# Second attention of a hybrid network: token routing in five units instead of four, the first two one tile later

## The reference, cut to what matters

```python
# L2, attention then experts, per batch
q, k, v = E @ WQ, E @ WK, E @ WV
# scores below the diagonal alone, softmax over the row, times v, added to E
# layer norm, then:
logits = xn @ gate_w + gate_b            # 128 -> 16
# two largest of 16, weights by softmax of the two
# each expert: silu(x @ w1) * (x @ w2) @ w3, summed with the two weights
```

## Time and profile before

| what | value |
|---|---|
| median of 3 timed runs | 1950.14 us (1949.3 to 1958.3) |
| the profiled execution's own time | 1943.94 us |
| its span in the profile | 1942.1 us |
| mean granted TensorE clock | 0.919 |
| PE busy | 1654.9 us, 85% |
| DVE busy | 1331.3 us, 69% |
| ACT busy | 991.6 us, 51% |
| POOL busy | 331.6 us, 17% |
| indirect DMAs of L1904 | 64, 62.1 us busy |

### The profile page before, as it was taken

How to read it: one execution, slowest core, us unless ns; L and a number is a source line. 1 busy time by engine, 2 the same in 40 slices (tenths; PEclk the granted TensorE clock), 3 DMA queues, 4 the chain that set the end, 5 groups by cost and what they waited for, 6 DMA issues and landing times. The chain is left out here.

```text
span 1942.1 us, 29755 instructions
## 1 busy us (share of the span) xinstructions
PE 1654.9 (85%) x9244; PEld 857.4 (44%) x9244; DVE 1331.3 (69%) x2650; ACT 991.6 (51%) x1857; POOL 331.6 (17%) x329
## 2 busy tenths in 40 slices
PE   5999897899999998598875199846999999996898
PEld 3777443222222223475554188722222222235576
DVE  5763598888888867345777244457888888856665
ACT  2555233366766775004444076642567676775233
POOL 6020400100000001100034545540000000011000
PEclk9999998699999999699998599966899999996899
DMA  3260057025454310104000132139033233310000
GB/s 105 98 143 10 0 150 221 1 49 86 75 87 74 70 48 16 25 1 138 1 23 30 55 97 68 41 133 248 17 57 57 56 56 56 56 37 2 6 17 22
DMA packets 117113, 122.71 MB, mean 63 GB/s; under 512 B 24300, under 2 KB 90324, under 8 KB 115976
## 3 DMA queue, kind: packets, MB, share of 16 engines
q1 hardware_dynamic: 101598, 102.07, 23.3%
q0 software_dynamic: 15408, 19.31, 3.5%
HBM read 79.00 MB, written 41.84 MB: 62 GB/s over the span
## 5 line engine op out<-in xcount | busy, mean ns | idle before, releaser
L944 DVE TENSOR_REDUCE heads_mx<-scales_n_bank 128x1 f32<-128x1024 f32 (+2 forms) x280 | 324.3, 1196 | 60.4 <-PE scales_n_bank L810 59.0
L925 ACT ACTIVATE heads_prob<-scales_t_bank 128x512 f32<-128x512 f32 x512 | 264.5, 603 | 140.2 <-PE scales_t_bank L829 140.2
L944 DVE TENSOR_REDUCE heads_mx<-edge_n_bank 128x1 f32<-128x1024 f32 x256 | 301.4, 1219 | 50.1 <-PE edge_n_bank L810 48.7
L925 ACT ACTIVATE heads_prob<-edge_t_bank 128x512 f32<-128x512 f32 x512 | 264.4, 603 | 133.2 <-PE edge_t_bank L829 133.1
L810 PE MATMUL scales_n_bank<-scale_ks,scale_qs 96*128 96x512 bf16 (+2 forms) x608 | 177.2, 382 | 27.5 <-DVE heads_mx L944 14.2
L810 PE MATMUL edge_n_bank<-edge_ks,edge_qs 99*128 99x512 bf16 x512 | 163.9, 404 | 23.8 <-PEq L43 12.8
L829 PE MATMUL scales_t_bank<-scale_qs,scale_ks 99*128 99x512 bf16 (+2 forms) x608 | 169.0, 365 | 3.6 <-ACT heads_prob L925 3.5
L829 PE MATMUL edge_t_bank<-edge_qs,edge_ks 102*128 102x512 bf16 x512 | 154.8, 382 | 3.5 <-ACT heads_prob L925 3.5
L845 PE MATMUL edge_o_bank<-heads_prob,edge_vs 128*32 128x512 f32 x1024 | 136.4, 605 | 0.1
L845 PE MATMUL scales_o_bank<-heads_prob,scale_vs 128*32 128x512 f32 x1024 | 136.4, 605 | 0.0
L810 PEld LDWEIGHTS scales_n_bank<-scale_ks,scale_qs 96*128 96x128 bf16 (+1 forms) x608 | 46.3, 99 | 174.8 <-issue 98.3
(11 more groups left out here) (365 smaller groups left out, 2700.4 us busy)
## 6 DMA issues: line engine op xcount, KB each, us to landing
edges_text<-edges_targets SPq DMA_DIRECT2D x16, 512.0 KB, 3.6
scale_qs<-scale_q_parts SPq DMA_DIRECT2D x60, 128.0 KB, 4.8
scale_ks<-scale_k_parts SPq DMA_DIRECT2D x60, 128.0 KB, 6.5
heads_wide<-heads_inverse_d POOLq DMA_DIRECT2D x15, 512.0 KB, 10.8
edge_qs<-edge_q_parts SPq DMA_DIRECT2D x48, 128.0 KB, 4.9
edge_ks<-edge_k_parts SPq DMA_DIRECT2D x48, 128.0 KB, 7.4
routed_x<-attn_zeros SPq DMA_DIRECT2D x2, 2600.0 KB, 15.2
experts_xs<-routed_x SPq DMA_DIRECT2D x16, 325.0 KB, 4.4
```

Of the source, the lines that this page charges most:

```text
L925: act.activation(to[:], t_ps[score_bank(of, place, g)[0]][0:TN, 0:HP * CH], ACT.Exp, scale=scale).then_inc(exped, 1)
L944: dve.tensor_reduce(mx[:, u % UC:u % UC + G], scores, AX.X, ALU.max, negate=True).then_inc(first_used, 1)
```

## The change

The routing is cut into five units instead of four. `COUNT` gives their tiles, `FIRST` their first tile. Units 0, 1 and 2 are batches 0, 1 and 2; units 3 and 4 are the two halves of batch 3, four tiles each.

- Units 0 and 1: every part stands one tile later than before, `place_rows` in tile 0 of the batch after. Their eight `normalise` are now four in tile 1 and four in tile 2, and the root alone is in tile 0.
- Unit 2: its parts stand where they stood, but its `place_rows` and `advance` stand ahead of `add_output` in the last tile, and its `note_pages` behind `measure(31)`.
- Unit 3 begins inside the loop: its root in tile 29, `find_shift` in tile 30, `normalise` and `turn_rows` in tile 30. Unit 4 is behind the loop.
- Units 3 and 4 turn their rows into the banks of the score buffer 0, which the last tiles have left free (`turned_ps`); unit 4 keeps its logits and sums in score buffer 1.
- `note_pages` is split: what the next unit needs (`base`, `last_shift`) is the new `advance`. `weigh` is split from `pick`.
- POOL waits once a unit, and scatters 16, 16, 16, 8 and 8 DMAs: 64 as before.

```diff
+    COUNT = [T] * (B - 1) + [T // 2, T // 2]
+    UNITS = len(COUNT)
+    FIRST = [sum(COUNT[:u]) for u in range(UNITS + 1)]
...
-        logits_ps, total_ps, within_ps = (x_ps[:, i * P:(i + 1) * P] for i in range(3))
+        turned_ps = lambda u: x_ps[:] if u < B - 1 else s_ps[0][:, (u - B + 1) * 512:(u - B + 2) * 512]
+        sums_ps = lambda u, i: (x_ps if u < B else s_ps[1])[:, i * P:(i + 1) * P]
...
-            for f in range(B):
-                pool.wait_ge(doubled, f + 1)
-                pool.wait_ge(armed, 2 * (f + 1))
-                pool.wait_ge(placed, f + 1)
-                for t in range(T):
+            for u in range(UNITS):
+                pool.wait_ge(doubled, u + 1)
+                pool.wait_ge(armed, 2 * (u + 1))
+                pool.wait_ge(placed, u + 1)
+                for t in range(COUNT[u]):
...
+            inside, behind = {}, {}
+            for u in range(B - 1):
+                begin = FIRST[u + 1]
+                if u < B - 2:
+                    behind[begin + 2] = (turn_rows, u, 0)
+                    inside[begin + 4], inside[begin + 5], inside[begin + 7] = (turn_rows, u, 1), (gate_logits, u), (count_picks, u)
+                else:
+                    behind[begin + 1] = (turn_rows, u, 0)
+                    inside[begin + 3], inside[begin + 4], inside[begin + 6] = (turn_rows, u, 1), (gate_logits, u), (count_picks, u)
+            behind[B * T - 2] = (turn_rows, B - 1, 0)
...
+            steps = {}
+            for u in range(B - 1):
+                begin = FIRST[u + 1]
+                if u < B - 2:
+                    steps[begin] = ((take_root, u),)
+                    steps[begin + 1], steps[begin + 2] = ((normalise, u, 0, 4),), ((normalise, u, 4, 8),)
+                    steps[begin + 5], steps[begin + 6], steps[begin + 7] = ((double, u),), ((take_odds, u),), ((arm, u),)
+                else:
+                    steps[begin], steps[begin + 1], steps[begin + 2] = ((take_root, u), (normalise, u, 0, 2)), ((normalise, u, 2, 4),), ((normalise, u, 4, 8),)
+                    steps[begin + 4], steps[begin + 5], steps[begin + 6] = ((double, u),), ((take_odds, u), (take_root, B - 1)), ((arm, u), (normalise, B - 1, 0, 4))
+            steps[B * T - 1] = ((take_rows, B - 1, 0), (double, B - 1))
...
+            def advance(u):
+
+                dve.tensor_tensor(base[u + 1][:], base[u][:], ends[u][:, E - 1:E], ALU.add)
+                then(dve.scalar_tensor_tensor(out=change[:], in0=fresh[:], scalar=0.0, in1=change[:], op0=ALU.is_gt, op1=ALU.mult))
+                then(dve.tensor_tensor(last_shift[:], last_shift[:], change[:], ALU.subtract))
...
-            beside = {0: (find_shift,), 4: (choose,), 5: (pick,), 6: (hand_out,), 7: (place_rows,)}
+            beside = {g: [] for g in range(B * T)}
+            for u in range(B - 1):
+                begin = FIRST[u + 1]
+                late = u < B - 2
+                beside[begin + late].append((find_shift, u))
+                beside[begin + 4 + late].append((choose, u))
+                beside[begin + 5 + late] += [(pick, u), (weigh, u)]
+                beside[begin + 6 + late].append((hand_out, u))
+                if late:
+                    beside[begin + 8] += [(place_rows, u), (advance, u)]
+                    beside[begin + 9].append((note_pages, u))
+            beside[B * T - 2].append((find_shift, B - 1))
+            beside[B * T - 1].append((note_pages, B - 2))
+            ahead = {B * T - 1: ((place_rows, B - 2), (advance, B - 2))}
...
+            choose(B - 1)
+            find_shift(B)
+            pick(B - 1)
+            hand_out(B - 1)
+            place_rows(B - 1)
+            weigh(B - 1)
+            advance(B - 1)
+            choose(B)
+            pick(B)
+            note_pages(B - 1)
+            hand_out(B)
+            place_rows(B)
+            weigh(B)
+            note_pages(B)
```

More of the change, by code:

```diff
@@ L1995, in _ @@
                     project(b + 1, early[t])
-                if b >= 1 and t in inside:
-                    inside[t](b - 1)
+                if g in inside:
+                    part, *which = inside[g]
+                    part(*which)
                 mix(g)
@@ L2000, in _ @@
                     project(b + 1, late[t])
-                if b >= 1 and t == 1:
-                    turn_rows(b - 1, 0)
-            turn_rows(B - 1, 0)
-            for part in inside.values():
-                part(B - 1)
+                if g in behind:
+                    part, *which = behind[g]
+                    part(*which)
+            gate_logits(B - 1)
+            count_picks(B - 1)
+            turn_rows(B, 0)
+            gate_logits(B)
+            count_picks(B)
             pe.wait_ge(tabled, 1)
@@ L2031, in keep_turned @@
                 act.activation(probT[g % 2][:, 0:t + 1, :], t_ps[:, 0:t + 1, :], ACT.Copy).then_inc(turn_kept, 1)
-            def take_root(f):
-                act.wait_ge(measured, (f + 1) * T)
-                if f >= 1:
-                    act.wait_ge(shifted, f)
-                act.activation(root[:], mv[:, f * T:(f + 1) * T, 1], ACT.Sqrt, bias=epsb[:]).then_inc(rooted, 1)
-            def normalise(f, first, end):
-                act.wait_ge(shifted, f + 1)
-                for t in range(first, end):
-                    act.activation(rows[:, f * T + t, 0, 0:C], m.tt[:, f * T + t, :], ACT.Identity, bias=shift[:, t:t + 1], scale=rstd[:, t:t + 1]).then_inc(normed, 1)
@@ new lines, in normalise, with take_rows @@
+            def normalise(u, first, end):
+                act.wait_ge(shifted, u + 1)
+                for t in range(first, end):
+                    act.activation(rows[:, FIRST[u] + t, 0, 0:C], m.tt[:, FIRST[u] + t, :], ACT.Identity, bias=shift[:, t:t + 1], scale=rstd[:, t:t + 1]).then_inc(normed, 1)
+            def take_rows(u, half):
+                done = FIRST[u] // 4 + half
+                act.wait_ge(x_turned, done + 1)
+                if u >= 1:
+                    act.wait_ge(logits_made, u if COUNT[u] == T else B - 1)
+                act.activation(xT[:, done % 2 * 512:(done % 2 + 1) * 512], turned_ps(u), ACT.Copy).then_inc(x_taken, 1)
@@ L2070, in _ @@
                 b, t = divmod(g, T)
-                f = b - 1
-                if b >= 1 and t == 2:
-                    take_rows(f, 0)
+                if g in fronts and t in (2, 3) and fronts[g][2] == 0:
+                    part, *which = fronts[g]
+                    part(*which)
                 keep_turned(g)
@@ L2149, in choose, with find_shift @@
-            def choose(f):
-                dve.wait_ge(logits_made, f + 1)
-                then(dve.tensor_tensor(logits[:], logits_ps.rearrange("p (t e) -> p t e", e=E), gb[:].rearrange("p (o e) -> p o e", o=1).broadcast_to((P, T, E)), ALU.add))
-                for t in range(T):
+            def find_shift(u):
+                n = COUNT[u]
+                dve.wait_ge(rooted, u + 1)
+                dve.wait_ge(measured, FIRST[u + 1])
+                if u >= 1:
+                    dve.wait_ge(normed, FIRST[u])
+                then(dve.reciprocal(rstd[:, 0:n], root[:, 0:n]))
+                dve.scalar_tensor_tensor(out=shift[:, 0:n], in0=mv[:, FIRST[u]:FIRST[u + 1], 0], scalar=-1.0, in1=rstd[:, 0:n], op0=ALU.mult, op1=ALU.mult).then_inc(shifted, 1)
@@ L2154, in choose @@
+            def choose(u):
+                n = COUNT[u]
+                dve.wait_ge(logits_made, u + 1)
+                then(dve.tensor_tensor(logits[:, 0:n, :], logits_ps(u)[:, 0:n * E].rearrange("p (t e) -> p t e", e=E), gb[:].rearrange("p (o e) -> p o e", o=1).broadcast_to((P, n, E)), ALU.add))
+                for t in range(n):
                     last = dve.max(top[:, t, :], logits[:, t, :])
                 then(last)
-                dve.tensor_tensor(gap[:], top[:, :, 1], top[:, :, 0], ALU.subtract).then_inc(compared, 1)
@@ L2183, in hand_out @@
+            def hand_out(u):
+                n = COUNT[u]
+                old, new, had, has = count[u % 2], count[1 - u % 2], room[u % 2], room[1 - u % 2]
+                dve.wait_ge(counted, u + 1)
+                then(dve.tensor_tensor_scan(filled[:, 0:E * n], segment[n][:].rearrange("p e t -> p (e t)"), total_ps(u)[:, 0:E * n], 0.0, ALU.mult, ALU.add))
+                then(dve.tensor_tensor(new[:], old[:], by_expert(filled, n)[:, :, n - 1], ALU.add))
                 dve.tensor_tensor(spare[:], had[:], old[:], ALU.subtract)
@@ L2234, in _ @@
                 invert(g)
+                for part, *which in ahead.get(g, ()):
+                    part(*which)
                 add_output(g)
```

230 lines of the change are left out of this document (110 added, 120 removed).

## The result

The changed kernel took 1945.81 us (median of 7 executions, 1941.46 to 1947.79) beside 1950.5 us of the kernel before on the same chip. The ratio is 0.9964, interval 0.9949 to 0.9979: -7.0 us, between -10 and -4. The interval excludes a ratio of 1, though the difference is under 0.5%. The forecast was -8.0. Taken of the 1950.14 us of before, the ratio gives 1943.1 us, where 1942.1 was forecast.

A forecast was written before the change was run, and what follows sets the result against it. In the loop no engine is full and waits pass round a ring; behind it POOL's scatters bound. The terms summed to -8.0 us (0.41%), from 1950.14 to 1942.1 us; 8 in 10 range 1936.5 to 1949.2.

The forecast's parts named there:

- Term 1: POOL's wait ahead of batch 3's scatters: gap closes, -3.0 us; two further waits for new units cost +0.5.
- Term 2: Last tile, from `hand_out` to `place_rows`: `add_output`, `measure` and a wait leave, -0.6 us.
- Term 3: Tile 30: unit 3's table load and root now stand ahead of ACT's copy, +1.3 us, +1.6 at most.
- term 4: Beginning of batch 1: PE no longer waits for unit 0's normalised rows, -3.2 us.
- term 5: Middle of batch 1: four transposes and eight logit products move a tile later on PE, -1.7 us.
- term 7: PE's half-clock stretches after waits: two waits go, at least one comes, -1.3 us, ends -3.1 and +2.
- Term 6: Batch 2: old stall goes, but `place_rows` and `advance` move into its tile 0; 0 us, ends -4.9 and +3.
- the slower rival: Batches 2 and 3: moved DVE work lies wholly on the path, PE at half clock behind; +14.8 us, chance 0.04.
- The rival with -12.9: Batch 2 gains as batch 1 does and the clock stays up: about 1936.5 us, chance 0.34.
- The rival in which the loop gains nothing: Loop over tiles: waits only move elsewhere and the gap alone closes; -1.8 us, 1948.3, chance 0.17.
- the 2.68 us of tile 18: Sign of being right: `mix` of tile 18, in batch 2, waits for ACT 2 us or more.
- the signs of being wrong: POOL waiting ahead of the last eight scatters, batch 2 as short as batch 1, or outside stages differing by microseconds.

The follow-up runs named there:

- experiment 2: Kernel before with its four units and old end; only units 0 and 1 routed one tile later. Ratio to the kernel before 0.9970.
- experiment 3: Changed kernel with unit 3's root moved behind the copy of tile 30 and behind `arm`. Ratio to the kernel before 0.9937.
- experiments 2 and 9: The second named: changed kernel with the edits of experiment 3 and experiment 7 together. 1936.23 us, ratio to the kernel before 0.9929.
- Experiment 6: Changed kernel with shift, root's use and normalising of units 0 and 1 back where the kernel before has them; transposes stay late. Ratio to the kernel before 0.9960.
- experiment 7: Changed kernel with `note_pages` moved behind `find_shift` in tiles 17 and 25. Ratio to the kernel before 0.9953.
- experiments 10 and 11: Changed kernel, then kernel before, each run once more unedited. Ratios to the kernel before 0.9964 and 1.0005.

## Why the prediction was right, and where it was not

The sum was -8.0, the stage gave -7.7 and the measurement -7.0. The gap, the last tile and the place of the loop's gain were right; that the sum came so near is in part luck, since the clock of the seventh term did not give its 1.3 us and the beginning of the loop gave more than was asked of it. Term by term:

- **Term 1.** Gap -3.0: exact, shown by POOL's rows and by experiment 2, where it stays. The two further waits: +0.5 forecast, 0 measured. Unit 3 came 17.2 us behind batch 2's slots (16 to 18 forecast), unit 4 at 26.5 (25 to 28). The 3 to 5 us to spare hold by the weights too, which the term left out (3.1 and 4.1).
- **Term 2.** -0.6 forecast; from tile 30 to the slots 7.4 us before, 6.6 after: -0.8.
- **Term 3 came out mis-sized.** +1.3 forecast, +2.9 measured (tile 29 to 30 takes 3.9 us before, 6.8 after); in experiment 3 the tile takes 3.9 again. The delay itself was forecast well: counted from `add_output` of tile 29, the copy starts at 0.85 us before and at 2.47 after, 1.6 later, and the `mix` at 2.07 and 3.42, 1.35 later; the rest was hidden behind `count_picks`, which held the `mix` before. The other 1.57 us are the `mix` at half clock, 3.30 us for 1.73. This cost stood in no part of the term. Its cause is shown in part: in all seven profiles with the early root the `mix` of tile 30 takes 3.20 to 3.36 us, and in four of the six without it 1.73 to 1.83; but in the other two, experiments 2 and 9, it takes 2.87 and 2.66 without any wait of its own. The root started 0.02 us behind its table load; the 1.38 us drain that the Trainium skill adds (ScalarE: Activation LUTs, What ACT_TABLE_LOAD costs) does not show.
- **Terms 4 and 5.** -4.9 forecast, -6.9 measured at tile 16. Tile 9 gives 1.5 and tile 10 3.1, in all 4.7 where term 4 had 3.2; up to tile 16 come 2.2 more (term 5: 1.7). In the 4.7 is the half-clock stretch at 932.8, which term 7 priced at 1.4 at most; I estimate 3.3 without it (4.7 less 1.4). Experiment 6 shows the cause named, PE's transposes behind the rows, for the 4.0 us up to tile 10; the four rows normalised ahead of the copy, of which term 4 spoke too, matter little.
- **Term 6.** 0 forecast, 0 measured, but in two pieces: batch 2 gives 1.9, batch 3 takes 1.9 back, 2.1 of it in its first tile, where `place_rows` and `advance` of unit 1 stand now and PE runs at 0.51 behind them. The prediction gave batch 3 a price in the slower rival alone. The `mix` of tile 18 did wait over 2 us, and its cause was cheaper to remove than thought (experiment 7: 2.9 us for 1.1 us of moved work).
- **Term 7 is the one that failed by its cause.** -1.3 forecast; outside the other terms nothing is left of it, and in all the clock gave about nothing. The term counted three half-clock stretches where the kernel before has four (the one at 973.7 was left out), and took at least one to come where two came. The stretches at 932.8 (it is inside the 6.9) and 973.7 went, the one of tile 18 stayed (980.6 before, 986.4 after), the long one of batch 3 stayed, and one came at 1020.5 and one in tile 30, which is inside term 3: four before, four after. By half of PE's busy time in each, as the term reckons, 1.4 and 1.6 us went and 1.7 and 1.6 came, an estimate.

So +1.6 in term 3 and about +1.3 in term 7 were set off by -2.0 in terms 4 and 5, -0.5 in term 1 and -0.2 in term 2. By cause, the 1.6 and some 1.4 of the 2.0 are clock as well. The rival with -12.9 did not happen, though experiments 3 and 7 together reach that figure with two moved lines. The rival in which the loop gains nothing is refuted by experiment 2. The slower one had its mechanism right, a lump of DVE work in tile 0 with a half-clock stretch behind it, at 2 us where it needed 11.5.

Of the signs, the 32 scatters without a gap, no wait of PE for rows in batches 1 and 2, DVE's 1.56 us wait for scores ahead of tile 11 (1.5 named) and the 2.68 us of tile 18 came as written. Of the signs of being wrong one came, stages outside differing by microseconds; experiments 10 and 11 show it to be the spread from one execution to the next, as far as they reach. Batch 2 (45.6 us from tile 16 to 24) did not become as short as batch 1 (40.4).

One sign could not be read as the prediction put it: "those slots 5 us earlier, near 1055.5". They came at 1065.04, yet 4.75 us earlier behind the mark.

## What to carry to other kernels

Where engines wait for each other in a ring, read the instruction on which one waits for a helper's product (here four transposes for normalised rows) and put that one behind the work it holds up; giving its producer more time mattered less here. Of the same work, put first what another engine waits for, and last what nobody needs soon. And compare stages by a mark at their own beginning when unedited stages differ between executions by more than the effect.

## What the runs showed of the hardware that was not expected

- A short wait of PE can be followed by as much again in lost clock. At 0.50, the same `mix` took 3.30 us instead of 1.73 and the one of tile 18 1.65 instead of 0.94; moving 1.1 us of work won 2.9. Which waits are followed by such a stretch was not predictable from their length here: 1.18 us in tile 30 was, 1.47 us in tile 18 of experiment 7 was not. Nor was a new wait needed: in experiments 2 and 9 the `mix` of tile 30 had none, and took 2.87 and 2.66 us. Waits of 1.18 and 1.92 us stand in tile 30 ahead of the `mix` in the changed kernel, in the one before and in experiment 3 alike, and in the last two the clock stayed up through it.
- The waits ahead of units 3 and 4 on POOL, three each with their semaphores up, added nothing that shows to the 1.27 us from scatter to scatter.
- The two kernels that were profiled twice repeat inside the stage to 0.4 us at worst, while the unedited part ahead of it (some 900 us) varies by 14 us over 13 executions.
